# Rotation partners of two cross attentions: VectorE's stream shuffle in place of a TensorE matmul, and new places in the hand-written order

## The chip, the cores and the metric

The kernel runs on one core of a Trainium2 chip. The metric is the device time of one execution in microseconds (us), and the number compared is the median over several runs. Before the change it is 2952.5 us (three runs, 2951.55 to 2956.18).

## The reference

A decoder of two layers on x of 8 batches x 512 tokens x 256 channels: band attention, cross attention, ternary feed-forward, self attention, cross attention, mixture of experts. The change touches the two cross attentions. The first, cut to what matters:

```python
q = (x_q @ W_q).reshape(B, Tq, H, D).transpose(0, 2, 1, 3)     # H = 16 heads of D = 16
kv = x_kv @ W_kv
k, v = (kv[..., :C], kv[..., C:])
...
def _rotate(x, sin, cos):
    x1 = x[..., ::2]
    x2 = x[..., 1::2]
    x1p = x1 * cos - x2 * sin
    x2p = x1 * sin + x2 * cos
    return jnp.stack((x1p, x2p), axis=-1).reshape(x.shape)
q = _rotate(q, sin_q, cos_q)
k = _rotate(k, sin_k, cos_k)
att = jnp.einsum('bhqd,bhkd->bhqk', q, k) / jnp.sqrt(jnp.asarray(D, x_q.dtype))
```

A masked softmax over the keys, a product with v and a projection follow. The second cross attention has biases, a window of 128 keys and the other usual form of the rotation, where the partner of channel d is d + 8 (of 16), not its neighbour. In both, each rotated row is its own row times a cosine plus its partner's row times a signed sine.

## The kernel before

Both cross attentions are written as one program for each engine. `spread_attention` (called cross0 here, about 277 to 790 us of the span) is the full one, `window_attention` (cross1, about 2157 to 2580 us) the one with the window. Activations lie with channels on the 128 partitions and the 512 tokens along the row. Channels are laid out so that one tile of 128 partitions holds eight half heads, and the q and the k rows of a batch are four such tiles, n = 1, 0, 3, 2 in that order (odd n is k, even n is q).

The work goes in **units**. In cross0 a batch has 32 units; a unit is an "exact" step (two matmuls of scores, keys on the partitions, whose exponential ScalarE takes from PSUM, line 444) and a "max" step (two matmuls of scores, queries on the partitions, whose row maximum VectorE takes, line 499), the max step running 13 units ahead. In cross1 a batch has 16 units, the max step is 8 ahead, and both steps begin with matmuls that write the window's bias (line 954, "cover"). The scores lie in PSUM in a ring of three buffers in cross0 (`SLOTS`) and two in cross1: TensorE writes a buffer again when ScalarE or VectorE has read what lay there. Everything else that TensorE does for a batch is put between the units, one or two pieces to a unit, and is called a **filler** here: products with the values ("value"), projections ("qk", "v", "out"), transposes of the normed tokens ("norm"), and transposes of the maxima ("mt"). Fillers write to another ring in PSUM, W, of two banks in cross0 and four in cross1 (`BANKS`); a filler waits until the one that held its bank has been read.

The order on each engine is not found by the hardware: the table `at` gives each step a place in units, and each engine's list is sorted by it. Its instructions run strictly in that order, and waits between engines are on counting semaphores. VectorE's steps in the W ring stand 0.3 units behind their place in the table (`soon`).

The rotation of one tile n takes these steps:

- "qk": two fp32 matmuls (lines 413, 1048; each appears as two records); ScalarE copies the result to `rows` (lines 467, 1111).
- "rot" on TensorE: an fp32 matmul of `rows` with the permutation `turnm` puts the partners' rows into a bank of W (lines 421, 1056; two records).
- "rot" on VectorE: `rsin` = partners x `sin` (lines 531, 1185).
- "rope" on GpSimd: `rows` x `cos` (600, 1255), plus `rsin` (604, 1259), for q in cross0 times a mask (612). The cosine product waits for `rsin`, since it overwrites `rows`, which the matmul must have read.
- "high" on ScalarE: a copy of the finished rows rounded to fp32r (473, 1118); GpSimd then subtracts it and keeps the rest (619, 1265). DMAs stack both parts into `qs` and `ks` ("stack"), from which the scores are made.

For the tile (0, 0), VectorE does GpSimd's part ("cosine", "rope", lines 535 to 546). The maxima reach `qs` by the steps "mt", a copy on ScalarE, one operation on VectorE (522) and four DMAs ("mdma"), and the first exact step of a group of heads waits for those.

## Time and profile before

| | |
|---|---|
| median of three runs | 2952.5 us |
| the profiled execution, its own time | 2952.8 us |
| its span, first to last instruction | 2951.0 us |
| mean granted TensorE clock | 0.957 |
| TensorE busy over the span | 2658.3 us (90%) |
| VectorE busy | 1945.2 us (66%) |
| ScalarE busy | 1399.1 us (47%) |
| GpSimd busy | 1107.2 us (38%) |

PE is TensorE's matmuls and PEld its weight loads, DVE is VectorE, ACT is ScalarE, POOL is GpSimd. The end of a matmul in the profile is modelled and laps over the next one's start, so what a matmul costs TensorE in a full stretch is read from start to start. Busy shares over the whole span say little here, because the stages have different limits; the two cross attentions have to be read by themselves.

### The profile page before, as it was taken

How to read it: one execution, taken by the hardware profiler on the slowest of the kernel's cores; microseconds unless marked ns; L12 is line 12 of the kernel's file. 1: busy time of each engine (PE TensorE's matmuls, PEld its weight loads, DVE VectorE, ACT ScalarE, POOL GpSimd, SP SyncE). 2: the span in 40 equal slices, each digit the busy share in tenths (PEclk: the TensorE clock that was granted, in tenths of full speed). 3: DMA queues.
4: the chain of work that ended last, by engine and by line, in shares of the span. 5: the costliest groups of instructions: out<-in, count | busy, mean ns of one | idle time of the engine just before them, and what ended most of it. 6: DMA issues, size and time to landing. Idle time of an engine off the chain costs nothing. (4 is left out here: it accounts for less than half of the span.)

```text
span 2951.0 us, 51682 instructions
## 1 busy us (share of the span) xinstructions
PE 2658.3 (90%) x17628; PEld 1631.8 (55%) x17629; DVE 1945.2 (66%) x3269; ACT 1399.1 (47%) x2199; POOL 1107.2 (38%) x854
## 2 busy tenths in 40 slices
PE   7997899999868899999999999999889999857998
PEld 4775333333235556565656565656544454456997
DVE  4776777877668765657575656666546666574555
ACT  2433466666558653434343434343335555443333
POOL 3233323233036343435343434343443333063333
PEclk9998799999879999999999999999989999958999
DMA  5002222222111000000000000000043232146666
GB/s 163 0 0 63 61 59 61 58 61 58 30 58 44 1 1 1 1 1 1 1 1 1 1 1 1 1 1 1 1 113 81 74 79 69 37 138 230 219 211 195
DMA packets 102982, 160.60 MB, mean 54 GB/s; under 512 B 28349, under 2 KB 63432, under 8 KB 97160
## 3 DMA queue, kind: packets, MB, share of 16 engines
q1 hardware_dynamic: 97784, 147.88, 17.5%
q0 software_dynamic: 3408, 8.46, 0.8%
q8 instruction: 133, 2.18, 0.3%
q10 hardware_dynamic: 1600, 1.61, 0.2%
q14 instruction: 57, 0.47, 0.1%
HBM read 91.79 MB, written 14.96 MB: 36 GB/s over the span
## 5 line engine op out<-in xcount | busy, mean ns | idle before, releaser
L1678 DVE TENSOR_REDUCE self_nmax<-self_SM 128x2 fp32r<-128x1024 f32 x256 | 313.3, 1224 | 211.7 <-PE self_SM L1567 211.7
L1656 ACT ACTIVATE self_PT<-self_ST 128x1024 f32<-128x1024 f32 x256 | 262.9, 1027 | 329.4 <-PE self_ST L1592 329.4
L1723 POOL TENSOR_TENSOR self_U<-self_PT 128x1024 f32<-128x1024 f32 x64 | 153.9, 2405 | 613.5 <-ACT self_PT L1656 613.5
L499 DVE TENSOR_REDUCE cross_nmax<-cross_S 128x2 f32<-128x1024 f32 x256 | 310.7, 1222 | 110.2 <-PE cross_S L347 109.2
L444 ACT ACTIVATE cross_PT<-cross_S 128x1024 f32<-128x1024 f32 x256 | 260.0, 1023 | 123.3 <-PE cross_S L358 121.4
L1726 POOL TENSOR_TENSOR self_U<-self_U,self_PT 128x1024 f32<-128x1024 f32 x128 | 303.4, 2371 | 31.9 <-ACT self_PT L1656 27.0
L1602 PE MATMUL self_W<-self_PT,self_V 128*64 128x512 f32 x1024 | 237.4, 606 | 19.6 <-ACT self_PT L1656 14.6
L1146 DVE TENSOR_REDUCE cross_nmax<-cross_S 128x4 f32<-128x1024 f32 x128 | 156.5, 1223 | 133.4 <-PE cross_S L967 133.3
L1698 DVE RECIPROCAL self_rcp<-self_W 128x512 f32<-128x512 f32 x64 | 214.7, 3354 | 33.8 <-PE self_W L1609 33.1
L1083 ACT ACTIVATE cross_PT<-cross_S 128x1024 f32<-128x1024 f32 x128 | 131.0, 1024 | 127.6 <-PE cross_S L983 127.4
L1602 PEld LDWEIGHTS self_W<-self_PT,self_V 128*64 128x64 f32 x1024 | 72.5, 139 | 161.4 <-issue 123.2
L358 PEld LDWEIGHTS cross_S<-cross_qs,cross_ks 51*128 51x128 f32 x512 | 49.2, 190 | 184.4 <-issue 119.0
L1660 ACT COPY self_Oraw<-self_W 128x512 f32<-128x512 f32 x64 | 37.6, 587 | 232.4 <-PE self_W L1602 232.4
L358 PE MATMUL cross_S<-cross_qs,cross_ks 51*128 51x512 f32 x512 | 131.3, 512 | 11.6 <-DMA cross_qs<-cross_mrow 5.8
L377 PE MATMUL cross_W<-cross_PT,cross_V 128*32 128x512 f32 x1024 | 140.9, 625 | 0.0
L1567 PE MATMUL self_SM<-self_k_hi,self_q_hi 64*128 64x512 f32 x512 | 114.8, 442 | 23.8 <-DVE self_nmax L1678 23.8
L600 POOL TENSOR_TENSOR cross_rows<-cross_rows,cross_cos 128x512 f32<-128x512 f32 x30 | 38.4, 1280 | 257.8 <-DVE cross_rsin L531 257.8
L347 PE MATMUL cross_S<-cross_ks,cross_qs 49*128 49x512 f32 x512 | 111.2, 431 | 11.2 <-ACT cross_PT L444 9.7
L3117 PE MATMUL moe_TR<-moe_W,moe_hid_hi 128*128 x312 | 114.8, 406 | 0.0
L3044 POOL TENSOR_TENSOR moe_hid_lo<-all_x,moe_hid_hi 128x512 fp32r<-128x512 f32 x40 | 58.5, 1462 | 141.7 <-ACT moe_hid_hi L3038 141.7
L1589 PE MATMUL self_ST<-self_q_hi,self_k_hi 64*128 64x512 f32 x512 | 105.6, 405 | 6.5 <-ACT self_PT L1656 5.2
L1567 PEld LDWEIGHTS self_SM<-self_k_hi,self_q_hi 64*128 64x128 f32 x512 | 48.6, 183 | 105.1 <-issue 50.5
(450 smaller groups left out, 7002.8 us busy)
## 6 DMA issues: line engine op xcount, KB each, us to landing
moe_staged<-in_L_ffn_W SPq DMA_DIRECT2D x36, 1024.0 KB, 6.1
cross_ks<-cross_parts SPq DMA_DIRECT2D x384, 64.0 KB, 2.3
cross_qs<-cross_parts SPq DMA_DIRECT2D x376, 64.0 KB, 2.3
all_x<-in_L_ffn_W SPq DMA_DIRECT2D x14, 1024.0 KB
all_x<-sorted_rows SPq DMA_DIRECT2D x83, 130.0 KB, 2.1
cross_cT<-in_ctx_T SPq DMA_DIRECT2D x16, 512.0 KB, 4.6
sorted_rows<-all_spare_row SPq DMA_DIRECT2D x1, 5460.0 KB, 23.8
all_x<-in_x SPq DMA_DIRECT2D x8, 512.0 KB, 4.0
```

Source lines behind the costliest of these rows:

```text
L358: m = pe.matmul(dst[:, r, :], ks[rows_r, p, k * P:(k + 1) * P], qs[rows_r, p, :], start=True, stop=True)
L377: m = pe.matmul(dst[32 * j:32 * j + 32, :], V[:, b % 2, k, 2 * p + r, :], PT[:, pt_slot[("exact", b, NT * p + k)], r, :], start=(k == 0), ...
L444: act.activation(PT[:, pt_slot[st], :, :], S[:, slot[st], :, :], ACT.Exp).then_inc(s_exped, 1)
L499: dve.tensor_reduce(nmax[:, g % 2, 0:R, n % PER_G], S[:, slot[st], :, :], AX.X, ALU.max, negate=True).then_inc(s_maxed, 1)
L1146: dve.tensor_reduce(nmax[:, g % 2, 0:R, n0:n0 + 2], S[:, slot[st], :, :].rearrange("p r (i c) -> p r i c", i=2), AX.X, ALU.max, negate=Tru ...
L1567: m = pe.matmul(SM[:, j, :], q_hi[at, c % SLOTS_QK, i * P:(i + 1) * P], k_hi[at, c % SLOTS_QK, :], start=True, stop=True)
L1602: m = pe.matmul(dst[j * D:(j + 1) * D, :], V[:, k, 2 * n + j, :], PT[:, k, j, :], start=(k == 0), stop=(k == NT - 1), skip_group_check=True)
L1656: act.activation(PT[:, k, :, :], ST[:, :, :], ACT.Exp).then_inc(exped.sem, 1)
L1678: dve.tensor_reduce(nmax[:, i, 0:P:D], SM[:, :, :], AX.X, ALU.max, negate=True).then_inc(maxed.sem, 1)
L1698: dve.reciprocal(rcp[:, :], bank_of(order, st)).then_inc(done, 1)
L1723: pool.tensor_tensor(U[:, c % 2, :, :], PT[:, 0, :, :], PT[:, 1, :, :], ALU.add).then_inc(added.sem, 1)
L1726: pool.tensor_tensor(U[:, c % 2, :, :], U[:, c % 2, :, :], PT[:, k, :, :], ALU.add).then_inc(added.sem, 1)
```

## The change

The TensorE step "rot" goes from both cross attentions, and with it `turnm`, its DMA and its bank of W. VectorE makes the partners' rows with one stream shuffle, which exchanges partitions p and p xor 16 within each block of 32. For cross0, whose partners were 2 partitions apart, the host orders the columns of W_q and W_k anew so that they are 16 apart. GpSimd's cosine product waits for the shuffle instead of for the product with the sine; its sum still waits for both. The table of places is new in nearly all lines, for both stages; two lines of it are shown.

```diff
-            at[("rot", b, n)] = o + t + 2.9
-            at[("rope", b, n)] = o + t + 3.0
-            at[("high", b, n)] = o + t + 5.6
+            at[("rot", b, n)] = o + t + 1.80
+            at[("rope", b, n)] = o + t + 0.50
+            at[("high", b, n)] = o + t + 7.20
...
-    RINGED = ("norm", "qk", "rot", "v", "out", "mt")
+    RINGED = ("norm", "qk", "v", "out", "mt")
...
+        PARTNER = [p ^ 16 for p in range(32)]
...
-                elif kind == "rot":
-                    dst = free_bank(st)
-                    pe.wait_ge(s_act, nth_act[("qk", b, n, KC - 1)])
-                    if b == 0:
-                        pe.wait_ge(s_rot, 48)
-                    pe.matmul(dst, turnm[:, :], rows[:, n % 2, :], start=True, stop=True).then_inc(s_full, 1)
...
                 elif kind == "rot":
                     if b == 0:
-                        dve.wait_ge(s_rot, 48)
-                    dve.wait_ge(s_full, nth_full[st])
+                        dve.wait_ge(s_rot, 32)
+                    dve.wait_ge(s_act, nth_act[("qk", b, n, KC - 1)])
                     before = ("rope", b, n - 2) if n >= 2 else ("rope", b - 1, n + 2)
                     if before in at:
                         roped(dve, *before[1:])
-                    dve.tensor_tensor(rsin[:, n % 2, :], src, sin[:, :], ALU.mult).then_inc(s_dve, 1)
+                    dve.stream_shuffle(rsin[:, n % 2, :], rows[:, n % 2, :], PARTNER).then_inc(s_shuffled, 1)
+                    dve.wait_ge(s_shuffled, nth_rot[st])
+                    dve.tensor_tensor(rsin[:, n % 2, :], rsin[:, n % 2, :], sin[:, :], ALU.mult).then_inc(s_dve, 1)
...
                         turned = row
-                        pool.wait_ge(s_dve, nth_dve[("rot", b, n)])
+                        pool.wait_ge(s_shuffled, nth_rot[("rot", b, n)])
                     pool.tensor_tensor(turned, row, cos[:, :], ALU.mult).then_inc(s_rope, 1)
                     pool.wait_ge(s_rope, base + 1)
-                    if (b, n) == (0, 1):
-                        pool.wait_ge(s_dve, nth_dve[("rot", b, n)])
+                    pool.wait_ge(s_dve, nth_dve[("rot", b, n)])
                     pool.tensor_tensor(row, turned, rsin[:, n % 2, :], ALU.add).then_inc(s_rope, 1)
...
-            for t, d in zip((turnm, sin, cos), rope[::-1]):
+            for t, d in zip((sin, cos), rope[::-1]):
```

How the order moves is shown at three places. First TensorE in cross0, batch after batch, around the projection of tile n = 2. L358 is the exact step, L347 the max step, L413 a half of the projection, L421 the rotation, L377 a value filler. Before:

```order
L413 MATMUL cross_W<-cross_hT,cross_wq 128x512
L358 MATMUL cross_S<-cross_qs,cross_ks 128x512 x2
L347 MATMUL cross_S<-cross_ks,cross_qs 128x512 x2
L421 MATMUL cross_W<-cross_rows,cross_turnm 128x512
L358 MATMUL cross_S<-cross_qs,cross_ks 128x512 x2
L347 MATMUL cross_S<-cross_ks,cross_qs 128x512 x2
L377 MATMUL cross_W<-cross_PT,cross_V 32x512 x4
```

In the changed kernel the same steps are L416, L361, L350 and L380:

```order
L416 MATMUL cross_W<-cross_hT,cross_wq 128x512
L361 MATMUL cross_S<-cross_qs,cross_ks 128x512 x2
L350 MATMUL cross_S<-cross_ks,cross_qs 128x512 x2
L361 MATMUL cross_S<-cross_qs,cross_ks 128x512 x2
L350 MATMUL cross_S<-cross_ks,cross_qs 128x512 x2
L380 MATMUL cross_W<-cross_PT,cross_V 32x512 x4
```

The rotation is gone; here one unit is left with no filler at all. In the rest of the batch the 32 large fillers (16 value, 8 qk, 4 v, 4 out) are spread to one a unit, apart from a few units that have two.

Second, VectorE in cross0 around the same kind of place. L499 is the maximum, L531 the product with the sine, L551, L553 and L555 what follows the value products of a group, L522 the maxima's row. Before:

```order
L499 TENSOR_REDUCE cross_nmax<-cross_S 128x2 x3
L531 TENSOR_TENSOR cross_rsin<-cross_W,cross_sin 128x512
L499 TENSOR_REDUCE cross_nmax<-cross_S 128x2 x3
L551 STREAM_TRANSPOSE cross_Ot<-cross_W 128x512
L553 RECIPROCAL cross_rinv<-cross_Ot 128x16
L555 TENSOR_TENSOR cross_On<-cross_Ot,cross_rinv 128x16x16
L499 TENSOR_REDUCE cross_nmax<-cross_S 128x2 x2
L522 SCALAR_TENSOR_TENSOR cross_mrow<-cross_mhi,cross_lows,cross_W 64x128
```

In the changed kernel:

```order
L496 TENSOR_REDUCE cross_nmax<-cross_S 128x2 x3
L528 STREAM_SHUFFLE cross_rsin<-cross_rows 128x512
L530 TENSOR_TENSOR cross_rsin<-cross_rsin,cross_sin 128x512
L496 TENSOR_REDUCE cross_nmax<-cross_S 128x2 x4
L550 STREAM_TRANSPOSE cross_Ot<-cross_W 128x512
L552 RECIPROCAL cross_rinv<-cross_Ot 128x16
L554 TENSOR_TENSOR cross_On<-cross_Ot,cross_rinv 128x16x16
L496 TENSOR_REDUCE cross_nmax<-cross_S 128x2
L519 SCALAR_TENSOR_TENSOR cross_mrow<-cross_mhi,cross_lows,cross_W 64x128
```

Two instructions stand between two maxima where one did, and the maxima's row comes one maximum sooner after a group.

Third, TensorE in cross1. L954 is the cover, L983 the exact step, L967 the max step, L1012 a value filler, L1056 the rotation, L1064 the projection of v. Before:

```order
L1012 MATMUL cross_W<-cross_PT,cross_V 32x128 x4
L1056 MATMUL cross_W<-cross_rows,cross_turnm 128x512
L954 MATMUL cross_S<-cross_band,all_ident_bf 64x512 x8
L983 MATMUL cross_S<-cross_qs,cross_ks 128x256 x4
L967 MATMUL cross_S<-cross_ks,cross_qs 128x256 x4
L1012 MATMUL cross_W<-cross_PT,cross_V 32x256 x4
L1064 MATMUL cross_W<-cross_wv,cross_cT 128x256 x4
```

In the changed kernel (L955, L984, L968, L1013, L1059; L1026 is a part of the output projection):

```order
L1026 MATMUL cross_W<-cross_wo,cross_OT 128x256 x2
L955 MATMUL cross_S<-cross_band,all_ident_bf 64x512 x8
L984 MATMUL cross_S<-cross_qs,cross_ks 128x256 x4
L968 MATMUL cross_S<-cross_ks,cross_qs 128x256 x4
L1059 MATMUL cross_W<-cross_wv,cross_cT 128x256 x2
L1013 MATMUL cross_W<-cross_PT,cross_V 32x256 x4
L955 MATMUL cross_S<-cross_band,all_ident_bf 64x512 x8
```

The projections of v and of the output, four matmuls in one unit before, are two in each of two units. On ScalarE, "high" stands two units further behind "qk": six exponentials lie between the copy to `rows` and it, where there were four.

## Rows read from the trace of the kernel before

**Rows 1.** Busy time of each engine by stretch (us, busy and count), clock, DMA.

```profile
300.00:340.00 40.00, 33.92 (x120) 12.22 (x122) 24.93 (x25) 14.18 (x19) 12.33 (x11) 0.62 0.18 45
...
380.00:740.00 360.00, 348.21 (x1894) 129.50 (x1893) 285.72 (x355) 229.74 (x287) 113.35 (x107) 1.00 0.24 60
2220.00:2520.00 300.00, 297.84 (x2792) 145.77 (x2784) 190.79 (x280) 157.02 (x215) 114.13 (x99) 1.00 0.30 75
```

**Rows 2.** Groups on TensorE (busy us, mean ns | idle before them): page, 380:740, 2180:2520.

```profile
L358 PE MATMUL cross_S<-cross_qs,cross_ks 51*128 51x512 f32 x512 | 131.3, 512 | 11.6 <-DMA cross_qs<-cross_mrow 5.8
...
L421 PE MATMUL cross_W<-cross_rows,cross_turnm 128*128 128x512 f32 x44 | 24.1, 630 | 2.5
...
L1056 PE MATMUL cross_W<-cross_rows,cross_turnm 128*128 128x512 f32 x56 | 31.5, 643 | 1.7 <-ACT cross_rows L1111 1.6
```

**Rows 3.** Timeline of cross0, 697 to 699 us (start, duration, engine, line).

```profile
696.96 0.40 PE L347 MATMUL cross_S<-cross_ks,cross_qs 49*128 49x512 f32 x2
...
697.40 1.23 DVE L499 TENSOR_REDUCE cross_nmax<-cross_S 128x2 f32<-128x1024 f32 x1 [0.50 <-PE cross_S L347]
...
697.47 1.10 PE L421 MATMUL cross_W<-cross_rows,cross_turnm 128*128 128x512 f32 x2
...
698.49 0.50 PE L358 MATMUL cross_S<-cross_qs,cross_ks 51*128 51x512 f32 x2
```

**Rows 4.** Timeline of TensorE in cross1, 2299 to 2304 us.

```profile
2299.58 1.12 PE L1056 MATMUL cross_W<-cross_rows,cross_turnm 128*128 128x512 f32 x2
2300.63 0.63 PE L954 MATMUL cross_S<-cross_band,all_ident_bf 64*64 64x512 bf16 x8
2301.19 0.50 PE L983 MATMUL cross_S<-cross_qs,cross_ks 50*128 50x256 f32 x4
2301.53 0.40 PE L967 MATMUL cross_S<-cross_ks,cross_qs 48*128 48x256 f32 x4
2301.85 0.64 PE L1012 MATMUL cross_W<-cross_PT,cross_V 128*32 128x256 f32 x8
2302.42 1.99 PE L1064 MATMUL cross_W<-cross_wv,cross_cT 128*128 128x256 f32 x8
```

**Rows 5.** Timeline of cross0's start, ScalarE and TensorE.

```profile
298.44 0.62 ACT L473 CAST cross_parts<-cross_rows 128x512 fp32r<-128x512 f32 x1 [5.18 <-POOL cross_rows L612]
...
299.70 1.34 PE L421 MATMUL cross_W<-cross_rows,cross_turnm 128*128 128x512 f32 x2 [2.99 <-ACT cross_rows L467]
...
325.72 0.80 PE L347 MATMUL cross_S<-cross_ks,cross_qs 49*128 49x512 f32 x2 [3.27 <-ACT cross_PT L444]
```

**Rows 6.** VectorE operations on 128 x 512: by group (busy us, mean ns), one by time.

```profile
L531 DVE TENSOR_TENSOR cross_rsin<-cross_W,cross_sin 128x512 f32<-128x512 f32 x28 | 19.1, 681 | 0.0
...
279.78 0.69 DVE L535 TENSOR_TENSOR cross_parts<-cross_rows,cross_cos 128x512 f32<-128x512 f32 x1 [7.05 <-ACT cross_rows L467]
...
L551 DVE STREAM_TRANSPOSE cross_Ot<-cross_W 128x512 f32<-128x512 f32 x26 | 18.3, 704 | 0.0
...
L1698 DVE RECIPROCAL self_rcp<-self_W 128x512 f32<-128x512 f32 x64 | 214.7, 3354 | 33.8 <-PE self_W L1609 33.1
...
L3041 DVE CAST moe_hid_hi<-all_x 128x512 fp32r<-128x512 f32 x40 | 17.1, 428 | 68.7 <-PE moe_TR L3118 68.6
```

**Rows 7.** Timeline, 281 to 285 us: VectorE and GpSimd with operands in SBUF.

```profile
281.22 1.27 POOL L604 TENSOR_TENSOR cross_rows<-cross_parts,cross_rsin 128x512 f32<-128x512 f32 x1 [1.86 <-DVE cross_rsin L531]
281.77 1.26 DVE L540 TENSOR_TENSOR cross_rows<-cross_parts,cross_rsin 128x512 f32<-128x512 f32 x1
...
283.07 0.69 DVE L543 TENSOR_TENSOR cross_rows<-cross_rows,cross_mall 128x512 f32<-128x512 f32 x1
...
283.26 1.62 POOL L619 TENSOR_TENSOR cross_parts<-cross_rows,cross_parts 128x512 fp32r<-128x512 f32 x1 [0.78 <-ACT cross_parts L473]
```

**Rows 8.** Timeline of VectorE, 642 to 645 us.

```profile
642.41 0.71 DVE L551 STREAM_TRANSPOSE cross_Ot<-cross_W 128x512 f32<-128x512 f32 x1
...
644.05 1.23 DVE L499 TENSOR_REDUCE cross_nmax<-cross_S 128x2 f32<-128x1024 f32 x1
```

204 lines of the change are left out of this document (100 added, 104 removed).

## The prediction

> **What bounds the kernel now.** I read the two stages first by stretch, because the change touches nothing else. In the full stretch of cross0 TensorE is busy 348.2 of 360 us and in that of cross1 297.8 of 300, both at a granted clock of 1.00 [rows 1]. VectorE has 285.7 of 360 (79%) and 190.8 of 300 (64%), ScalarE 64% and 52%, GpSimd 31% and 38%. So TensorE sets the pace in both, with 3% and 1% of slack, and what leaves its queue shortens the stage, as long as no other engine takes its place. Next I read the groups on TensorE, to see what little it does wait for [rows 2], then the timeline around one rotation in each stage [rows 3, 4], since a matmul's modelled end laps over the next start. Last I read the start of cross0, the only place where TensorE stands idle for microseconds because of this very step [rows 5].
>
> **The matmul that goes.** In cross0 a max step starts at 696.96 and its two matmuls take 0.33 (0.34 and 0.32 for the same pair of steps in cross1, start to start [rows 4]), so TensorE is free at 697.29. The rotation starts at 697.47 and the next exact step at 698.49 [rows 3]. The rotation thus costs 1.20 us: 1.02 of work, and 0.18 in which it waits, with its weights not yet in place. In cross1 it takes 1.05 from start to start [rows 4], and the group's idle time is small, 1.7 us for 28 rotations [rows 2]. There are 4 tiles x 8 batches = 32 rotations a stage. Of these 4 a stage belong to the first batch, before the full stretch, so I count 28 x 1.20 = 33.6 us in cross0 and 28 x 1.05 = 29.4 us in cross1.
>
> **The start.** In cross0's start TensorE stands 2.99 us before one rotation and then works some 1.3 us on it, because ScalarE's copy to `rows` stood behind a "high" that had waited 5.18 us for GpSimd [rows 5]. Without the matmul, TensorE goes on to the max steps queued behind it. I count 4.3 us for this one. The other first rotations lie on the chain from projection to stack: matmul and product gave about 1.1 + 0.7, and shuffle and product about 0.7 + 0.7, with the cosine product beside the latter. I count 1 us for each stage. Sum 6.3 us.
>
> **The new places.** "high" two units on means that ScalarE no longer stands at the head of its queue for GpSimd's mask product with exponentials behind it; TensorE felt that once clearly, 3.27 us waiting for an exponential [rows 5]. I count those 3 us. "mt" stands one filler sooner, so the DMAs of the maxima land about 1 us sooner; exact steps waited 5.8 us for them over cross0 [rows 2], of which I take half, 3 us. On the other side, the sooner "mt" takes the free bank of W, and the filler behind it then needs the bank of the value products, which VectorE must have transposed. From the end of a value filler (1.02) an exact and a max step (0.67) and the short "mt" pass on TensorE, while VectorE, free of the maximum before it about 0.25 us after that end, transposes for 0.70 [rows 6] and is done at 0.95: a stall of 0 to 0.3 us, more where VectorE runs late, once or twice a batch. In the unit that is left without a filler the ring can wait as well. I take 0.5 us a batch, 4 us in all, as a loss.
>
> **VectorE's price.** 64 shuffles come in. The trace has none. The nearest row is the stream transpose, 704 ns for 128 x 512; below stands a plain fp32 cast from SBUF at 428 ns, above the reciprocal at 3354 ns [rows 6]. I take 0.70, since the transpose is the only other operation that carries rows across partitions. The Trainium skill ("VectorE: DVE Perf Modes", the perf-mode tier table) gives a shuffle of 2048 elements about 2400 ns whatever the permutation; a quarter of that would be 0.6 us, an estimate by that page, and the sum would not change by it. The product with the sine now reads SBUF instead of PSUM: 690 ns for such a product against 681 [rows 6], so nothing. VectorE in cross0 would have 285.7 + 22 x 0.70 = 301 us (22 rotations lie in that stretch [rows 2]) in a stretch shortened by 22 x 1.20 to about 334 us: 90%. That is high, so the queue has to be looked at, not only the share.
>
> What stands behind the shuffle on VectorE is the next maximum, and TensorE waits for that maximum two units later, three buffers on. From the end of a max step: VectorE starts 0.11 later [rows 3] and gives its buffer back after 1.14 (0.09 of the 1.23 laps over the next). TensorE needs that buffer after filler, unit, filler: 1.02 + 0.67 + 1.02 = 2.7 us. If a lump L comes between two maxima, the second is done at 1.25 + L + 1.14, and it is wanted at 1.69 + 2.7 = 4.4, so L up to 2.0 us costs nothing. The trace bears that out: transpose, reciprocal and product hold the next maximum back by 644.05 - 642.41 = 1.64 us [rows 8]. Shuffle and product are 1.40. In cross1 (two buffers) a unit with one filler is 0.56 + 0.34 + 0.32 + 0.57 + 1.0 = 2.8 us [rows 4], the buffer is wanted 1.9 after the max step, and L may be 2.3. So the shuffle is hidden behind TensorE in both, by 0.6 and 0.9 us. Without that cover it would cost 0.7 x 64 = 45 us.
>
> The wait of VectorE on ScalarE's copy is new, too: behind it stand the maxima. The copy is made right behind one exponential, and VectorE has a maximum of 1.2 us before it comes to the shuffle, so I count nothing.
>
> **The product beside GpSimd.** The cosine product of GpSimd and the sine product of VectorE now become ready at the same moment, both with two operands in SBUF. The rows show what happens then: VectorE's sum, started 0.55 us into one of GpSimd's, took 1.26 instead of 0.69 and ended 0.54 after it; GpSimd's subtraction, started 0.19 behind VectorE's product, took 1.62 instead of 1.27 [rows 6, 7]. Who starts second waits. The Trainium skill ("SBUF — State Buffer", two separate sides) says the same as a rule: the shared pair of ports is held by whoever starts first for the whole instruction. VectorE has no other engine's signal to wait for and should start first; then GpSimd pays some 0.5 us x 62, on an engine busy a third of the time, which stands on no path. If VectorE comes second, its lump is 0.70 + 1.26 = 1.96, at the edge of the 2.0 above.
>
> **Sum.** 33.6 + 29.4 + 6.3 + 3 + 3 - 4 = 71 us. The profiled execution took 2952.8 us, which is 0.3 over the median of 2952.5; so about 2882 us.
>
> **Rivals.**
> *VectorE costs part of it in cross0.* For it: 90% busy, and places where another short operation lies beside the pair (nearest rows 0.43 and 0.68 [rows 6]), or where GpSimd has the ports; both together make a lump of 2.4 to 2.6 us against 2.0. Against it: VectorE catches up 0.5 us in each unit (1.69 against 1.14). Price 0.4 to 0.9 us x 32, with the middle at 20 us: 2902 us.
> *The clock.* In cross0's start the granted clock was 0.62 over 40 us, that is, mostly the lower of the two levels, after TensorE had stood idle for the waits of [rows 5]; the full stretches have 1.00 [rows 1]. If those idle times shrink and the fall does not come, TensorE gains at most 40 x 0.38 = 15 us: 2867. If instead one more such stretch comes, in a start that is thinner without its rotations, the same 15 us are lost: 2897.
> *No change.* The matmul was only filling time in which TensorE would have waited for the exponential or the maximum. Against it: a buffer is read at 1.25 us and wanted at 2.7, so with one filler a unit there are 1.4 us of room in cross0, and nearly every unit keeps one. 2950.
> *Slower: the shuffle is a slow instruction.* One mechanism: it goes the way of the reciprocal, 3.35 us. Lump 4.03, of which 2.0 is free in cross0 and 2.3 in cross1; stalls 2.0 and 1.7 us x 32 = 120 us, so 2882 + 120 = about 3000. It decides from a shuffle of about 1.45 us free (mean) + 71/64 = 2.6 us on. Against it: the transpose does as much moving in 0.70.
>
> **Chances.** Forecast 0.60 (own range 2868 to 2893); VectorE's part or a colder clock 0.21 (2893 to 2930); a better start 0.09 (down to 2850); no change 0.04; slower 0.06. The range that leaves out at most 2 in 10 reaches into both neighbours: 2858 to 2912. A difference of 0.2% (6 us) is about what a measurement of this kernel can tell from none. Faster 0.90, same 0.04, slower 0.06.
>
> **What the profile after would show.** TensorE without the two rotation lines, cross0's full stretch some 36 us and cross1's 31 us shorter, both with TensorE still above 94% busy; shuffles of 0.6 to 0.8 us; VectorE near 90% in cross0; GpSimd's cosine product grown from 1.27 to about 1.8 us and the sine product still 0.7; shorter ScalarE waits for GpSimd before "high". It is wrong if TensorE waits tens of microseconds for the maxima (the shuffle is not hidden), if the shuffle takes over 2 us, or if the clock has new stretches at the lower level.

## The result and the profile after

| | before | after |
|---|---|---|
| median, us | 2952.9 (4 runs, 2951.55 to 2956.18) | 2882.5 (4 runs, 2879.65 to 2889.64) |
| ratio after / before | | 0.9764, 95% interval 0.9744 to 0.9784 |
| span of the profiled execution | 2951.0 | 2877.8 |
| mean granted TensorE clock | 0.957 | 0.963 |

The change makes the kernel 2.4% faster. The page of the changed kernel gives for each engine busy time, share of the span and instructions:

```profile
PE 2586.4 (90%) x17485; PEld 1604.6 (56%) x17501; DVE 1991.7 (69%) x3397; ACT 1391.1 (48%) x2199; POOL 1131.3 (39%) x854
```

TensorE has lost 71.9 us of busy time and VectorE has gained 46.5. The busy time by stretch (us, busy and count of TensorE, weight loads, VectorE, ScalarE, GpSimd; granted clock; DMA), for the stretches that answer to [rows 1]; they are cut where the shorter stages now end:

```profile
300.00:340.00 40.00, 33.43 (x135) 12.35 (x134) 32.49 (x39) 18.12 (x24) 15.11 (x12) 0.74 0.21 54
394.00:680.00 286.00, 277.29 (x1580) 104.36 (x1576) 258.30 (x349) 198.07 (x254) 105.11 (x93) 1.00 0.26 65
2110.00:2440.00 330.00, 320.66 (x3007) 154.61 (x3005) 242.07 (x377) 174.40 (x248) 154.30 (x121) 0.99 0.33 81
```

In cross0 VectorE is busy 258.3 of 286 us, which is 90%; it was 79% before [rows 1]. TensorE is at 97%, as before the change. The groups on VectorE and GpSimd (count | busy us, mean ns | idle time before them) in 394 to 680 us are:

```profile
L496 DVE TENSOR_REDUCE cross_nmax<-cross_S 128x2 f32<-128x1024 f32 x155 | 186.6, 1220 | 25.5 <-PE cross_S L350 24.1
...
L528 DVE STREAM_SHUFFLE cross_rsin<-cross_rows 128x512 f32<-128x512 f32 x19 | 14.1, 740 | 0.0
L530 DVE TENSOR_TENSOR cross_rsin<-cross_rsin,cross_sin 128x512 f32<-128x512 f32 x19 | 13.2, 692 | 0.7
L599 POOL TENSOR_TENSOR cross_rows<-cross_rows,cross_cos 128x512 f32<-128x512 f32 x19 | 32.7, 1724 | 84.3 <-DVE cross_rsin L528 84.3
```

The shuffle takes 740 ns (727 in cross1), the product with the sine 692 as in [rows 6], and GpSimd's cosine product 1724.

**Where the 73.2 us of the span came from.** I cut each stage at the start of the exact step of unit 0 of each batch. Two such rows, one batch apart, of the kernel before, from TensorE's timeline (start, duration):

```profile
507.94 0.50 PE L358 MATMUL cross_S<-cross_qs,cross_ks 51*128 51x512 f32 x2
...
572.02 0.50 PE L358 MATMUL cross_S<-cross_qs,cross_ks 51*128 51x512 f32 x2
```

And of the changed kernel:

```profile
491.14 0.50 PE L361 MATMUL cross_S<-cross_qs,cross_ks 51*128 51x512 f32 x2
...
550.32 0.50 PE L361 MATMUL cross_S<-cross_qs,cross_ks 51*128 51x512 f32 x2
```

A batch of cross0 took 64.08 us here and takes 59.18. All eight starts of each stage, with the start of TensorE's first transpose in the stage and the end of its last output product, give this:

| stretch | before | after | difference |
|---|---|---|---|
| cross0, first transpose to the first batch's unit 0 | 44.9 | 41.3 | -3.6 |
| cross0, first batch's unit 0 to the last one's | 444.6 | 410.3 | -34.3 |
| cross0, from there to the last output product | 65.3 | 55.6 | -9.7 |
| between the two stages (not touched) | 1324.7 | 1321.3 | -3.4 |
| cross1, first transpose to unit 0 | 41.8 | 39.0 | -2.8 |
| cross1, first batch's unit 0 to the last one's | 345.2 | 324.4 | -20.8 |
| cross1, the rest | 42.6 | 44.8 | +2.2 |

The 3.4 us between the stages are no effect of the change: in the profiled executions of all fourteen kernels this part took 1320.8 to 1328.4 us. The point forecast was 2882 and the time is 2882.5, but the parts do not agree: the prediction has 40.9 us for cross0 (33.6 + 5.3 + 3 + 3 - 4) and 30.4 for cross1 (29.4 + 1); the table has 47.6 and 21.4. The experiments ask how much of each is the matmul and how much is the table of places. Their measure is the **period**, the time from one batch's unit 0 to the next one's in the steady part of a stage; it repeats within some 0.05 us from batch to batch in most kernels, apart from batches that hold a stretch of lower clock, which are 1 to 5 us longer and are spoken of where they matter.

### The profile page after: what moved, and what is told of

Same layout as the page of the kernel before. It is cut to its first block and busy times, and to the rows that moved or that the text cites. A ratio compares the mean times of both kernels' runs of the same rounds, so it can differ in the third digit from the quotient of the medians.

```text
span 2877.8 us, 51533 instructions
## 1 busy us (share of the span) xinstructions
PE 2586.4 (90%) x17485; PEld 1604.6 (56%) x17501; DVE 1991.7 (69%) x3397; ACT 1391.1 (48%) x2199; POOL 1131.3 (39%) x854
## 5 line engine op out<-in xcount | busy, mean ns | idle before, releaser
L380 PE MATMUL cross_W<-cross_PT,cross_V 128*32 128x512 f32 x1024 | 135.8, 604 | 0.0
L361 PEld LDWEIGHTS cross_S<-cross_qs,cross_ks 51*128 51x128 f32 x512 | 48.2, 186 | 154.1 <-issue 92.1
L361 PE MATMUL cross_S<-cross_qs,cross_ks 51*128 51x512 f32 x512 | 126.7, 493 | 8.1 <-DVE cross_nmax L496 4.9
L350 PE MATMUL cross_S<-cross_ks,cross_qs 49*128 49x512 f32 x512 | 110.0, 429 | 10.8 <-ACT cross_PT L441 6.4
L1613 PE MATMUL self_W<-self_wo,self_OT 128*128 128x256 f32 x448 | 98.6, 380 | 7.0 <-DVE self_OT L1698 7.0
```

The costliest lines, as they stand in the source:

```text
L361: m = pe.matmul(dst[:, r, :], ks[rows_r, p, k * P:(k + 1) * P], qs[rows_r, p, :], start=True, stop=True)
```

## The experiments

All of them in one table; periods are in us a batch. Each ratio is to runs of the kernel before on the same chip.

| kernel | period cross0 | period cross1 | median | ratio (95%) |
|---|---|---|---|---|
| before | 64.06 | 49.94 | 2952.9 | |
| after | 59.20 | 47.24 | 2882.5 | 0.9764 (0.9744 to 0.9784) |
| old_places | 63.26 | 49.57 | 2952.3 | 0.9993 (0.9979 to 1.0007) |
| matmul_new_places | 62.27 | 51.09 | 2934.5 | 0.9924 (0.9908 to 0.9941) |
| no_shuffle | 58.64 | 47.24 | 2880.4 | 0.9739 (0.9723 to 0.9756) |
| shuffle_2 | 61.2 | 47.55 | 2906.5 | 0.9853 (0.9824 to 0.9882) |
| cos_waits | 59.2 | 47.24 | 2881.8 | 0.9760 (0.9741 to 0.9780) |
| high_early | 59.56 | 47.23 | 2886.2 | 0.9765 (0.9749 to 0.9781) |
| cross1_merged | 59.2 | 50.20 | 2906.3 | 0.9829 (0.9810 to 0.9849) |
| spread_fillers | 70.8 to 77.8 | 48.45 | 2994.5 | 1.0144 (1.0118 to 1.0170) |
| spread_mt | 62.7 to 64.4 | 48.45 | 2943.9 | 0.9966 (0.9951 to 0.9981) |
| old_places_no_shuffle | 62.81 | 48.55 | 2937.1 | 0.9939 (0.9917 to 0.9960) |
| matmul_twice | 67.20 | 53.36 | 3002.4 | 1.0160 (1.0135 to 1.0185) |
| mt_last | 59.2 | 46.86 | 2878.2 | 0.9738 (0.9722 to 0.9754) |

The kernels old_places_no_shuffle and matmul_twice ran twice, the others four times or more. In no_shuffle and old_places_no_shuffle the rotation is not the reference's.

### The two halves of the change: old_places and matmul_new_places

old_places is the changed kernel with both whole tables of places of before. Two of the lines:

```diff
-            at[("rope", b, n)] = o + t + 0.50
-            at[("high", b, n)] = o + t + 7.20
+            at[("rope", b, n)] = o + t + 3.0
+            at[("high", b, n)] = o + t + 5.6
```

> The changed kernel (shuffle, cosine product waiting for the shuffle) with the table of places of the kernel before in both stages. Read by the period from batch to batch, which was 64.06 us in cross0 and 49.94 in cross1 before, and is 59.2 and 47.24 in the changed kernel. Theory (the TensorE work that left is the gain): cross0 59.3 to 60.5, cross1 45.8 to 47, since the matmul cost 4.8 and 4.1 us a batch and no new changes between kinds of matmul come in; total 2870 to 2890. Rival (the new places earn the gain, the shuffle alone runs VectorE's queue into TensorE): cross0 62 or more, total 2915 or more.

matmul_new_places is the kernel before with the new tables, the matmul standing as far behind its projection as it did:

```diff
+            at[("rot", b, n)] = o + t + 2.90
```

> The kernel before, with its rotation matmul, and the new table of places; the rotation stands where it stood behind its projection. Theory: the table alone earns little in the full stretch: cross0 about 64 a batch, cross1 about 51.4 (47.24 + 4.14), total 2945 to 2970. Rival (the places earn most of it): total 2920 or less.

The theory for old_places fell. The shuffle alone gives 0.8 and 0.4 us a batch, and nothing in the median: 2952.3 us. The new tables alone give 1.8 us a batch in cross0 and cost 1.15 in cross1; their median, 2934.5, lies between what the theory and the rival said. Together the two halves give 4.86 and 2.70. So the two halves do not add: in the new tables the matmul's going is worth 3.07 and 3.85 us a batch, in the old ones 0.80 and 0.37, where the prediction counted 4 x 1.20 = 4.8 and 4 x 1.05 = 4.2 whatever the table.

The 0.8 and 0.4 us a batch of old_places do not reach its median, because other batches are longer. The first two of cross1 took 51.66 and 52.52 us, against 49.01 and 49.93 before the change, and one batch of cross0 took 66.38. From the first unit 0 to the last, cross0 took 445.3 us against 444.6, and cross1 348.5 against 345.2. In those batches the granted clock was lower. The rows of old_places (columns as above) for that batch of cross0 and for the two of cross1:

```profile
566.30:632.70 66.40, 61.23 (x332) 22.97 (x328) 54.38 (x73) 40.93 (x52) 21.65 (x19) 0.95 0.23 58
2189.60:2293.80 104.20, 96.18 (x878) 46.93 (x874) 66.38 (x106) 52.58 (x72) 44.14 (x36) 0.93 0.29 70
```

The same two batches of cross1 before the change:

```profile
2193.70:2292.60 98.90, 96.95 (x892) 46.64 (x888) 60.88 (x94) 52.51 (x72) 41.12 (x36) 0.98 0.29 73
```

It is not a matter of one execution: the mean granted clock was 0.952 to 0.956 in the ten runs of old_places and 0.957 to 0.962 in the thirteen of the kernel before on the same chip. That TensorE's new waits bring the lower clock about fits this, but was not tested by itself.

Where the time stays in old_places is seen in its timeline. First TensorE in cross0, at the unit that has lost its rotation:

```profile
549.03 0.40 PE L350 MATMUL cross_S<-cross_ks,cross_qs 49*128 49x512 f32 x2
549.32 0.49 PE L361 MATMUL cross_S<-cross_qs,cross_ks 51*128 51x512 f32 x2
550.36 0.50 PE L350 MATMUL cross_S<-cross_ks,cross_qs 49*128 49x512 f32 x2 [0.54 <-ACT cross_PT L441]
```

Between two max steps (L350) there is only the exact step (L361), and the next max step waits 0.54 us for an exponential, since the buffer into which it writes is still being read. The same in cross1, with ScalarE's exponential:

```profile
2300.21 1.02 ACT L1078 ACTIVATE cross_PT<-cross_S 128x1024 f32<-128x1024 f32 x1 [0.30 <-PE cross_S L984]
2300.33 0.43 PE L1013 MATMUL cross_W<-cross_PT,cross_V 128*32 128x128 f32 x8
...
2301.28 0.85 PE L955 MATMUL cross_S<-cross_band,all_ident_bf 64*64 64x512 bf16 x8 [0.53 <-ACT cross_PT L1078]
2302.06 0.51 PE L984 MATMUL cross_S<-cross_qs,cross_ks 50*128 50x256 f32 x4
```

The exponential runs from 2300.21 to 2301.23, and the cover that needs its buffer starts at 2301.28. The unit has only a small filler, so TensorE is there 0.5 us early and then waits for VectorE's maximum too (0.78 us pass from 2301.28 to the exact step at 2302.06, against 0.56 in [rows 4]). The groups' idle time shows how much of this there is. The max steps of cross0 before the change (380 to 740 us) and the cover of cross1 (2220 to 2480):

```profile
L347 PE MATMUL cross_S<-cross_ks,cross_qs 49*128 49x512 f32 x358 | 73.5, 405 | 5.9 <-ACT cross_PT L444 4.9
...
L954 PE MATMUL cross_S<-cross_band,all_ident_bf 64*64 64x512 bf16 x672 | 53.0, 388 | 1.9 <-DVE cross_nmax L1146 1.3 <-ACT cross_PT L1083 0.6
```

In old_places (380 to 720, and 2220 to 2480 us):

```profile
L350 PE MATMUL cross_S<-cross_ks,cross_qs 49*128 49x512 f32 x340 | 72.5, 421 | 25.2 <-ACT cross_PT L441 24.9
...
L955 PE MATMUL cross_S<-cross_band,all_ident_bf 64*64 64x512 bf16 x664 | 60.3, 398 | 14.2 <-ACT cross_PT L1078 9.1 <-DVE cross_nmax L1141 4.6
```

In the changed kernel, over 394 to 680 us:

```profile
L350 PE MATMUL cross_S<-cross_ks,cross_qs 49*128 49x512 f32 x310 | 63.7, 407 | 4.0 <-ACT cross_PT L441 3.5
```

In cross0 the idle time before the max steps is 5.9 us in 5.6 batches before the change (1.1 a batch), 25.2 in 5.4 in old_places (4.7), and 4.0 in 4.8 in the changed kernel (0.8): 3.6 of the 4.0 us a batch that are missing in old_places. Most of it, 2.6 a batch, stands behind the four units that have lost their filler (0.5 to 0.7 each). The rest, 1.9 against 0.8 before, stands at two units where ScalarE waited for GpSimd ahead of "high"; spread_mt below shows that wait. In cross1 the idle time goes from 0.4 to 2.7 a batch in this stretch, and to 2.0 in the two batches from 2343 us on, which have no lower clock; in these the cover also takes 1.5 us a batch more from start to start. Together that is 3.5 of the 3.8 us missing there. So most of the matmul's time lay over waits which, without it, appear in its place. That is the prediction's rival "no change", for the old tables: true there in size, wrong for the change as it was made.

### What the shuffle costs: no_shuffle, shuffle_2, cos_waits

no_shuffle leaves the shuffle out, so each row is added to its own sine product and not to its partner's:

```diff
-                    dve.stream_shuffle(rsin[:, n % 2, :], rows[:, n % 2, :], PARTNER).then_inc(s_shuffled, 1)
-                    dve.wait_ge(s_shuffled, nth_rot[st])
-                    dve.tensor_tensor(rsin[:, n % 2, :], rsin[:, n % 2, :], sin[:, :], ALU.mult).then_inc(s_dve, 1)
+                    dve.tensor_tensor(rsin[:, n % 2, :], rows[:, n % 2, :], sin[:, :], ALU.mult).then_inc(s_dve, 1)
+                    dve.wait_ge(s_dve, nth_dve[st])
+                    dve.sem_inc(s_shuffled, 1)
```

> The changed kernel without its 64 shuffles: VectorE multiplies the rows themselves, not their partners, by the sine, so the rotation is not the reference's. Theory (the shuffle is hidden behind TensorE): cross1 unchanged at 47.2 a batch, cross0 at most 0.5 shorter than 59.2, total within 6 us of the changed kernel. Rival (VectorE's queue costs part of the gain in cross0): cross0 1 us a batch shorter or more, total 10 to 20 us lower.

shuffle_2 issues each shuffle twice, one behind the other:

```diff
+                    for again in range(1):
+                        dve.wait_ge(s_shuffled, 2 * (nth_rot[st] - 1) + again + 1)
+                        dve.stream_shuffle(rsin[:, n % 2, :], rows[:, n % 2, :], PARTNER).then_inc(s_shuffled, 1)
```

> The changed kernel with every shuffle made twice in a row (the same result), so that 2.2 us stand between two maxima where 1.43 do. Theory (up to 2.0 us is free in cross0 and 2.3 in cross1, and leaving the shuffle out gave 0.56 us a batch in cross0 and nothing in cross1): cross0 0.8 to 2 us a batch longer, since VectorE is then at 95%, cross1 unchanged at 47.2; total 2888 to 2900. Rival (VectorE is the bound in cross0 already): cross0 2.9 us a batch longer, total 2905 or more; cross1 longer too.

cos_waits puts the cosine product back behind the sine product:

```diff
-                        pool.wait_ge(s_shuffled, nth_rot[("rot", b, n)])
+                        pool.wait_ge(s_dve, nth_dve[("rot", b, n)])
```

> The changed kernel, with GpSimd's cosine product waiting for VectorE's sine product again instead of for the shuffle alone. Theory (GpSimd stands on no path): its product takes 1.27 instead of 1.72 us, the chain of a rotation gets about 0.3 us longer, period unchanged within 0.2 us, total within 4 us of 2882. Rival (the earlier start is what lets the copy of the rotated rows find them ready): 0.5 us a batch or more, total 2890 or more.

Four shuffles a batch are 3.0 us of VectorE's time. Taken away, they give back 0.56 us a batch in cross0 and nothing in cross1 (the median moves by 2 us, which its spread does not tell from none). So the shuffle is hidden, by four fifths in cross0 and wholly in cross1. A second one costs 2.0 of its 3.0 us in cross0 and 0.3 in cross1, and 24 us in all, more than I had expected. In that kernel, 394 to 680 us:

```profile
394.00:680.00 286.00, 268.61 (x1530) 100.59 (x1528) 261.94 (x375) 192.16 (x245) 99.87 (x89) 1.00 0.25 63
```

VectorE is at 92%, only 2 points above its 90%, and TensorE has fallen from 97% to 94%: in a steady batch its exact steps now wait 2.2 us for VectorE's maxima. A lump of 2 x 0.74 + 0.69 = 2.17 us is above the 2.0 that the prediction called free in cross0 and below the 2.3 of cross1. The bound by lumps was about right, and 90% left hardly any room.

cos_waits is the same as the changed kernel in both periods. Its cosine product, no longer beside the sine product:

```profile
L599 POOL TENSOR_TENSOR cross_rows<-cross_rows,cross_cos 128x512 f32<-128x512 f32 x19 | 24.5, 1287 | 98.1 <-DVE cross_rsin L530 98.1
```

It takes 1287 ns against 1724. Started 0.7 us sooner and run 0.44 us longer, the product gains 0.25 us for the chain, and nobody waits for it. That edit of the wait is worth nothing.

### "High" back where it was: high_early

```diff
-            at[("high", b, n)] = o + t + 7.20
+            at[("high", b, n)] = o + t + 5.60
```

> The changed kernel with ScalarE's copy of the rotated rows back at 5.6 units behind the projection in cross0 instead of 7.2; cross1 as in the changed kernel. Theory (two units on keeps ScalarE from standing for GpSimd's mask product with exponentials behind it; TensorE felt little of it before): cross0 0.3 to 1 us a batch longer, total 2885 to 2892. Rival (this is what makes the new table work): cross0 2 us a batch longer or more, total 2900 or more.

0.36 us a batch in cross0, 2.9 us over eight batches; the medians differ by 3.7. The size is what the prediction counted (3 us), but spread over all batches and not in the start, which takes 41.3 us with either place. This is the price of the place of "high" with everything else new; with the rotation at its old place it is another (spread_mt).

### Do the new places work by one filler a unit? cross1_merged, spread_fillers, spread_mt, old_places_no_shuffle

My first theory for cross1 was another. The halves of "v" and "out", one unit apart in the new table, cost more than together, so merging them should pay:

```diff
-                at[("v", b, m, part)] = o + t + part
+                at[("v", b, m, part)] = o + t + 0.05 * part
...
-                at[("out", b, m, part)] = o + t + part
+                at[("out", b, m, part)] = o + t + 0.05 * part
```

> The changed kernel, with the two halves of each projection of v and of the output in one unit of cross1 as before, not in two. In cross1 the changed kernel saves 2.70 us a batch, though the rotation took 4.14. Theory (the rest is lost to more changes between kinds of matmul: a piece of four costs 1.06 us, a piece of eight 1.93 to 1.99): 0.8 us a batch shorter, 46.4, total 6 us lower. Rival (one filler a unit is what keeps the rings fed): units without one wait for VectorE, period 47.3 or longer, total the same or higher.

The theory fell. A batch of cross1 becomes 3.0 us longer (50.20), and 4.1 and 4.4 in two batches that hold a stretch of lower clock: what merging saves on TensorE is small beside the waits of the units that it leaves thin. The rival, one filler a unit, held, but the wait is for ScalarE's exponentials (2.6 us a batch before the cover, none in the changed kernel), not for VectorE as it said.

spread_fillers then gives the old tables only this part of the new ones:

```diff
-        for m, ts in enumerate(((-14.4, -12.8), (1.6, 3.2))):
+        for m, ts in enumerate(((-4.50, -1.50), (3.80, 6.30))):
...
-        for m, ts in enumerate(((41.6, 42.0), (43.2, 43.25))):
+        for m, ts in enumerate(((42.80, 43.40), (53.00, 54.50))):
...
-        for n, t in zip(QK_ORDER, (-24.0, -20.0, -16.0, -12.0)):
+        for n, t in zip(QK_ORDER, (-23.80, -20.00, -17.00, -10.80)):
...
-                at[("v", b, m, part)] = o + t + 0.4 + 0.3 * part
+                at[("v", b, m, part)] = o + t + part
...
-                at[("out", b, m, part)] = o + t + 0.3 * part
+                at[("out", b, m, part)] = o + t + part
```

> The changed kernel (shuffle) with the table of before, except the places of TensorE's fillers: the halves of the projections of v and of the output in both stages, and in cross1 those of q, k and the norm, stand as in the new table, so that nearly every unit has one large filler. ScalarE's copy of the rotated rows, the rotation, the stacks and the maxima's rows stand as before. With the old table alone the kernel took 2952 us, 63.26 us a batch in cross0 and 49.57 in cross1. Theory (a unit that loses its filler waits for its ring, so the freed time is only got by spreading the rest): cross1 47.2 or a little less a batch, cross0 60 to 61.5, total 2885 to 2910. Rival (ScalarE standing for GpSimd in the copy of the rotated rows is what holds cross0): cross0 stays above 62.5.

The theory did not come out in either stage. In cross1 the new places do about half: 49.57 to 48.45, of the 2.33 us between old_places and the changed kernel. In cross0 they do harm: 71 to 78 us a batch, with a granted clock of 0.88 over three of these batches. TensorE and VectorE there:

```profile
497.15 0.41 PE L367 MATMUL cross_W<-all_ident,cross_nmax 128*32 128x128 f32 x4
...
498.16 1.13 PE L416 MATMUL cross_W<-cross_cT,cross_wk 128*128 128x512 f32 x2
...
500.93 0.32 DVE L519 SCALAR_TENSOR_TENSOR cross_mrow<-cross_mhi,cross_lows,cross_W 64x128 fp32r<-64x128 f32 x1
...
501.30 1.13 PE L393 MATMUL cross_W<-cross_wo,cross_OT 128*128 128x256 f32 x4 [2.02 <-DVE cross_mrow L519]
```

The second filler of W behind the "mt" (L367) is the output projection, which needs the "mt"'s bank, and VectorE gives it free only with the maxima's row (L519) at 501.25: 2.02 us. The mean granted clock of the run was 0.943, against 0.963 in the changed kernel, so part of the 71 to 78 us is the clock's. So in the ring of two banks the place of "mt" and the place of the projections go together. spread_mt moves it:

```diff
-            at[("mt", b, g)] = o + PER_G * g - 4.1
-            at[("mdma", b, g)] = o + PER_G * g - 3.0
+            at[("mt", b, g)] = o + PER_G * g - 4.80
+            at[("mdma", b, g)] = o + PER_G * g - 4.50
```

> The kernel spread_fillers (shuffle, old table, fillers of the new one) with cross0's maxima transposes and their DMAs also where the new table has them, 0.7 and 1.5 units sooner. In spread_fillers cross0 went to 71 to 78 us a batch. Theory (with two banks, a transpose of the maxima that stands right before a half projection keeps its bank until VectorE has made the maxima's row, and the next filler waits up to 2 us for it; one filler sooner that wait is hidden): cross0 falls to 59.5 to 61.5 a batch, total about 2890 to 2905, cross1 as in spread_fillers, 48.45. Rival (something else of the new table holds cross0, the place of the copy of the rotated rows or of the rotation): cross0 stays above 65.

It takes back some 10 us a batch, down to 62.7 to 64.4 (67.4 in one with a stretch of lower clock), but 3.5 to 5 us above the changed kernel remain. So neither the theory's 59.5 to 61.5 nor the rival's 65 came out. The max steps in 380 to 680 us of spread_mt:

```profile
L350 PE MATMUL cross_S<-cross_ks,cross_qs 49*128 49x512 f32 x298 | 63.0, 418 | 24.1 <-ACT cross_PT L441 23.8
```

24.1 us in 4.7 batches are 5.1 a batch, against 0.8 in the changed kernel: what remains is a wait for the exponential's buffer again. It is not the one of a unit without a filler: in a batch it stands at three units, 0.70 us behind the one unit that has no filler, as in the changed kernel, and 2.37 and 1.70 at two others. ScalarE and TensorE at the first of these:

```profile
577.43 1.16 POOL L610 TENSOR_TENSOR cross_rows<-cross_rows,cross_mall 128x512 f32<-128x512 f32 x1
...
578.62 0.62 ACT L470 CAST cross_parts<-cross_rows 128x512 fp32r<-128x512 f32 x1 [2.95 <-POOL cross_rows L610]
...
579.14 1.93 ACT L441 ACTIVATE cross_PT<-cross_S 128x1024 f32<-128x1024 f32 x2
...
580.31 0.50 PE L350 MATMUL cross_S<-cross_ks,cross_qs 49*128 49x512 f32 x2 [2.37 <-ACT cross_PT L441]
```

ScalarE stands 2.95 us ahead of "high" (L470) until GpSimd's mask product (L610) is done, with two exponentials behind it, and the max step waits for the first of them. Ahead of "high" ScalarE waits 6.3 us a batch in spread_mt and in old_places, 4.8 in the kernel before, and not at all in the changed kernel. TensorE's two waits behind it, 4.07 us, are about as much as remains. The kernel high_early had "high" at its old place too and lost only 0.36, so another of the old places must make GpSimd's rows late. The nearest are the rotation's: in the new table "rot" stands 1.1 units and "rope" 2.5 units sooner. That is argued from the table and was not tried, nor were the places of "qk", "stack", "back", "stat" and the transposes in cross0.

old_places_no_shuffle asks whether in old_places the shuffle ate the gain; it has the old tables, and no_shuffle's edit on top, with the same part left out.

> The kernel before's table, without the matmul and without the shuffle (VectorE multiplies the rows themselves by the sine, so the rotation is not the reference's): the least work that any engine can have. Theory (under the old table the unit that loses its filler waits for its ring of score buffers, whatever VectorE does): cross0 62.5 or more a batch, cross1 49 or more, total 2935 or more. Rival (it is the shuffle in VectorE's queue that takes the gain back under the old table): cross0 59 to 61, cross1 46 to 47.5, total below 2900.

62.81 and 48.55: with neither matmul nor shuffle the old tables give 1.25 and 1.39 us a batch of the 4.8 and 4.2 counted. That is the theory's side, though cross1 came out a little under its 49. In the old tables the shuffle costs 0.45 and 1.0 us a batch, 0.56 and 0 in the new: less in cross0, more in cross1. So most of the missing gain is waiting that belongs to the order, and a smaller part is the shuffle.

### The price of the matmul itself: matmul_twice

The kernel before with each rotation matmul issued twice:

```diff
+                    pe.matmul(dst, turnm[:, :], rows[:, n % 2, :], start=True, stop=True)
```

> The kernel before with every rotation matmul made twice in a row (the same result). Theory (TensorE bounds both stages under the old table while every unit has its filler, and a rotation costs 1.02 to 1.05 us of work): 4.1 us a batch more in each stage, 68.2 and 54.1, total about 3020. Rival (a part of the time behind the matmul is a wait for the rings that more work would fill): clearly less than 4.1 a batch.

+3.14 and +3.42 us a batch for four more matmuls, 0.79 and 0.86 each. That is less than the 4.1 of the theory, but not because waits swallow the work. One pair in cross1, with the cover behind it:

```profile
2390.81 1.12 PE L1057 MATMUL cross_W<-cross_rows,cross_turnm 128*128 128x512 f32 x2
2391.77 1.02 PE L1058 MATMUL cross_W<-cross_rows,cross_turnm 128*128 128x512 f32 x2
2392.73 0.63 PE L955 MATMUL cross_S<-cross_band,all_ident_bf 64*64 64x512 bf16 x8
```

From start to start the two take 1.92 us, where one takes 1.05 [rows 4]: a second matmul right behind its like adds 0.86 or 0.87, and four of them are the whole 3.42. TensorE has no idle time in a steady batch of cross1 in either kernel, so there was nothing to swallow. In cross0 a pair takes 1.88 against 1.02, 3.4 a batch, and the idle time falls from 2.1 to 1.8; so waits take 0.3 of it. The rival thus holds for less than a tenth in cross0 and not at all in cross1.

Work added to TensorE in the order before is paid in full or nearly so, and work taken out of the same places returns 0.2 and 0.1 us a matmul with the shuffle in its stead (old_places), 0.3 in both without it (old_places_no_shuffle). Both are true at once: TensorE hardly waits, and the rings behind it are nearly as tight as it is.

### Where the last of cross1 went, and a better version: mt_last

In the changed kernel's cross1 TensorE waits for nothing in a steady batch, and a batch is still only 2.70 us shorter and not 4.2. Start-to-start sums of the same work in a steady batch of each kernel say where: "v" 3.86 before and 4.25 now, "out" 3.84 and 4.25, the value fillers 7.81 and 8.32, the rest about 0.1. Together 1.4 us. Four rows of the changed kernel show the pattern:

```profile
2291.16 0.41 PE L998 MATMUL cross_W<-all_ident,cross_nmax 128*32 128x128 f32 x4
2291.50 1.13 PE L1059 MATMUL cross_W<-cross_wv,cross_cT 128*128 128x256 f32 x4
2292.57 0.64 PE L1013 MATMUL cross_W<-cross_PT,cross_V 128*32 128x256 f32 x8
2293.13 0.63 PE L955 MATMUL cross_S<-cross_band,all_ident_bf 64*64 64x512 bf16 x8
```

Half of "v" costs 1.07 from start to start (both halves in one go cost 1.93 before), and the value filler before the cover costs 0.56, while before "mt" it costs 0.45. So what a piece costs depends on its neighbours: 0.1 us more for a value filler ahead of the cover than ahead of "mt", 0.2 more for a projection in two pieces than in one. "mt" stands ahead of the half projection; behind the value filler it would spare that filler the dearer neighbour in each of the four groups. mt_last:

```diff
-            at[("mt", b, g)] = o + PER_G * g - 3.80
-            at[("mdma", b, g)] = o + PER_G * g - 3.50
+            at[("mt", b, g)] = o + PER_G * g - 3.34
+            at[("mdma", b, g)] = o + PER_G * g - 3.20
```

> The changed kernel with the transposes of the maxima in cross1 placed last in their unit, behind the value filler, not ahead of a projection. In the trace, a value filler ahead of one of these transposes takes 0.45 us and ahead of a projection or a cover 0.57, and TensorE has no idle time in cross1's full stretch. Theory (the full stretch of cross1 is the sum of its pieces and of the changes between kinds): 46.8 us a batch, total 2 to 4 us under the changed kernel. Rival (the maxima's row comes too late for its buffer or its bank): cross1 over 47.24.

The same place in mt_last:

```profile
2293.15 1.13 PE L1059 MATMUL cross_W<-cross_wv,cross_cT 128*128 128x256 f32 x4
2294.22 0.64 PE L1013 MATMUL cross_W<-cross_PT,cross_V 128*32 128x256 f32 x8
2294.67 0.39 PE L998 MATMUL cross_W<-all_ident,cross_nmax 128*32 128x128 f32 x4
2294.99 0.41 PE L955 MATMUL cross_S<-cross_band,all_ident_bf 64*64 64x512 bf16 x4
```

The value filler costs 0.45, "mt" 0.32, and the period falls by 0.38 us. All of it is in the value fillers, which take 0.5 us a batch less; "mt" takes 0.1 more. A part is that the changed kernel cuts one value filler a batch in two by an "mt", which mt_last does not. The median is 2878.2 (2876.29 to 2880.11), the best of all kernels with the whole computation; its ratio's interval overlaps that of the changed kernel, so the period shows the gain and the median only fits it (8 x 0.38 = 3.0 us, 4.3 measured).

## Why the prediction was right, and where it was not

The forecast was right in sign and in size (71 us counted, 70.4 measured between medians). That it fits to the microsecond is luck: its errors cancelled. By its steps:

- **"What leaves its queue shortens the stage, as long as no other engine takes its place."** This is the step that failed. It priced the matmul at its start-to-start time because TensorE had only 3% and 1% of slack [rows 1]. With the old tables, 4.8 and 4.2 us a batch came out as 0.8 and 0.37 (old_places). No other engine had become the bound by its share; the units that had lost their filler waited for their own ring of score buffers. The prediction named that wait only in half a sentence, under the new places, and put 0.5 us a batch on it with the new bank wait. Its argument against "no change" (room of 1.4 us "with one filler a unit") held for units with a filler, and the unit in question has none. TensorE's small slack was read rightly: a matmul more does cost its full 0.86 us in cross1 (matmul_twice). What does not follow is that one matmul less gives it back.
- **"The new places": +3, +3 and -4 us, some 2 in all.** Mis-sized by far. From old_places to the changed kernel the tables are worth 4.06 and 2.33 us a batch, and 70 us of the median (2952.3 to 2882.5); the periods make 45 of these in seven intervals a stage, the rest lies at the stages' starts and ends and in batches with a lower clock. What they do in cross1 is, for about half, one filler a unit (spread_fillers); in cross0 that part works only with a new "mt", and what then remains is ScalarE's wait for GpSimd ahead of "high" (spread_mt). The 3 us for "high" were right in size by high_early, but not in place, and with the rotation at its old place the wait that this term priced costs 4.07 us a batch (spread_mt). The 5.8 us of waits for the DMAs of the maxima fell to 0.4, where half was counted; 3.3 of them had stood in the last batch. The 0.5 us a batch for the rings was too little: in a steady batch of the changed kernel TensorE waits 0.70 us behind the unit without a filler, and 0.34 + 0.18 for a bank of W, behind the maxima's row and not behind the values' transpose as the prediction had it. Where "mt" is wrongly placed such a wait is 2 us (spread_fillers).
- **The matmul, 33.6 and 29.4 us.** The middle of cross0 gave 34.3 and that of cross1 20.8. In cross0 the figure fits by chance: the matmul's part in the new tables is 3.07 a batch, and the tables' own 1.80 comes on top. The steady batches gave 4.86 each, the first interval 3.2 and the last 6.7. In cross1 its part is 3.85, but the tables alone cost 1.15, mostly for the dearer neighbours that the halving of "v" and "out" brought, which the prediction did not price.
- **The start, 6.3 us, and 3 for "high" there.** Measured: 3.6 in cross0 and 2.8 in cross1 to unit 0, 6.4 together. So the 5.3 us of cross0 were 3.6, and the 3 for "high" did not show there. The wait ahead of the rotation did not go either: TensorE now stands 3.52 us ahead of a projection for ScalarE's copy to `rows`, and its idle time up to the second batch's unit 0 is 22 us, where it was 21, with waits for VectorE's maxima of up to 2.0 us where the longest was 0.5. What went is the work of the first rotations. The low clock did not go, it came sooner: 0.74 in 300 to 340 us against 0.62 [rows 1], but 0.73 in 270 to 300 against 0.89. Over 270 to 340 us it is 0.74 against 0.73, so the clock rival gained nothing in the start.
- **The end of cross0** was not in the sum, and gave 9.7 us. The row for it, from the last batch's unit 0 on, before the change (columns as above):

```profile
761.90:827.20 65.30, 55.42 (x310) 20.69 (x306) 33.86 (x43) 32.82 (x36) 0.00 (x0) 0.87 0.05 13
```

  and in the changed kernel:

```profile
723.70:779.30 55.60, 50.12 (x310) 20.20 (x306) 34.36 (x44) 32.70 (x36) 0.00 (x0) 0.97 0.09 22
```

  The same 310 matmuls are busy for 5.3 us less, which the clock can account for (65.3 x 0.13 less 55.6 x 0.03 is 6.8 us at most), and TensorE's idle time falls from 9.9 to 5.5 us. The largest part of that are two waits for the DMAs of the maxima's row, 3.3 us before and 0.4 now; that the sooner "mdma" takes them away is likely and was not tested alone.
- **The shuffle, 0.70 us, hidden.** Right: 0.74 and 0.73, and its removal gives 0.56 and 0 us a batch. The page of the Trainium skill that the prediction named ("VectorE: DVE Perf Modes", the perf-mode tier table) gave 0.6 by estimate; the transpose's row was nearer. VectorE at 90% in cross0 was right to the point, and "VectorE costs part of it" held for 0.56 x 8 = 4.5 us of the 20 that the rival had.
- **Lump free up to 2.0 us in cross0 and 2.3 in cross1.** shuffle_2 with 2.17 costs 2.0 us a batch in cross0 and 0.3 in cross1, which has the order right. The first is more than 4 x 0.17 = 0.7, so the free lump in cross0 is less than 2.0, or it is smaller where other short operations stand beside it; and in cross1 a lump under the 2.3 was not quite free.
- **The ports.** GpSimd's cosine product 1.72 us, from 1.27, and the sine product at 0.69: as forecast. The Trainium skill's rule ("SBUF — State Buffer", two separate sides) agrees with this trace in this: the second to start is the one that grows. By its wording the second waits until the first is done; here it grew by 0.45 us where VectorE's product had 0.58 left to run. The timeline of one such pair:

```profile
696.51 0.75 DVE L528 STREAM_SHUFFLE cross_rsin<-cross_rows 128x512 f32<-128x512 f32 x1
...
697.29 0.69 DVE L530 TENSOR_TENSOR cross_rsin<-cross_rsin,cross_sin 128x512 f32<-128x512 f32 x1
...
697.40 1.73 POOL L599 TENSOR_TENSOR cross_rows<-cross_rows,cross_cos 128x512 f32<-128x512 f32 x1 [4.75 <-DVE cross_rsin L528]
```

  VectorE starts 0.11 us ahead and pays nothing; GpSimd pays 0.45.

What stays open: which of the new places has the rotated rows ready for "high" in cross0, "rot" and "rope" being the nearest; how much of the lower clock in old_places comes from TensorE's own waits; and what the other half of the tables' 2.33 us in cross1 is.

## What to carry to other kernels

An engine that is 97 to 99% busy may be the bound for work that is added and still give back little for work that is taken out: in cross1 a matmul more cost its full 0.86 us, and a matmul less gave 0.1, or 0.35 with nothing in its stead. Before pricing a removal at its duration, take the instruction out of its place in the order, and ask when the next instruction's buffer is free. If the instruction fills a gap that a ring of buffers imposes, its going is worth only what remains, until the rest of the work is laid out anew. Price the removal and the new order together, as one term, and test them as two halves each alone. When a wait is for a buffer, look one engine further: in cross0 the late exponential was ScalarE standing for GpSimd, and not a missing filler. Where the order is by hand, halving a piece or changing what stands next to it costs a little on TensorE each time, which start-to-start sums by kind show and idle time does not.

## What the runs showed of the hardware that was not expected

- What a piece costs TensorE depends on its neighbours, and the difference is listed as idle nowhere. In cross1 half a projection of "v" takes 1.07 us from start to start and the whole in one go 1.93 (not 2.14); a value filler takes 0.45 before "mt" and 0.56 before the cover; a rotation matmul takes 1.05 alone, and a second one behind it adds 0.86 or 0.87 (matmul_twice).
- VectorE's shuffle of 128 x 512 fp32 took 0.74 us in cross0 and 0.73 in cross1, near the stream transpose (0.70) and far from the reciprocal [rows 6].
- GpSimd's product is slowed from 1.29 to 1.72 us by a VectorE product of 0.69 that starts 0.11 ahead of it, that is, by about two thirds of that product's length.
